# A gate carried with each sorted row, and half of the combine moved beside the last expert

## What is computed

```
mod = (silu(c) @ wmod).reshape(16, 6, 1, 128)      # sa, ca, ga, sb, cb, gb for each sequence
gb  = (2 * (gb >= 0) - 1) * maximum(abs(gb), 0.25)
h = layernorm(x) * (1 + cb) + sb
out = swiglu(h, shared_gate_up, shared_down)
probs = softmax(h @ gate_weight.T)                 # 8 experts
top_p, sel = top_k(probs, 2); top_p /= sum(top_p) + 1e-8
out += sum over the 2 picks: top_p * swiglu(h, experts_gate_up[sel], experts_down[sel])
x = x + gb * out
```

## Time and profile before

| | us |
|---|---|
| median of 3 runs | 767.89 (766.65 to 770.26) |
| the profiled execution, its own time | 766.81 |
| its span, first to last instruction | 765.0 |
| mean granted TensorE clock over the span | 0.933 |
| busy in the span: PE, DVE, ACT, POOL | 659.7, 561.0, 431.9, 375.5 |
| first part, up to the first expert tile | 0 to 401 |
| 19 expert tiles | 401 to 728 |
| last turn, last scatters, combine, output | 728 to 765 |

### The profile page before, as it was taken

How to read it: one execution, slowest core, us unless ns; L and a number is a source line. 1 busy time by engine, 2 the same in 40 slices (tenths; PEclk the granted TensorE clock), 3 DMA queues, 4 the chain that set the end, 5 groups by cost and what they waited for, 6 DMA issues and landing times.

```text
span 765.0 us, 11950 instructions
## 1 busy us (share of the span) xinstructions
PE 659.7 (86%) x3026; PEld 502.2 (66%) x3026; DVE 561.0 (73%) x1233; ACT 431.9 (56%) x822; POOL 375.5 (49%) x299
## 2 busy tenths in 40 slices
PE   5777989889998989888679999999999999999900
PEld 2455766666676667666458787778878777887800
DVE  4878978979798987976656676766776676776736
ACT  3456657575666658563345565556666665566600
POOL 1324545738456464736245473829246273832245
PEclk9797989999899999999989999999999999999955
DMA  8403001010000000000221303030401303010045
GB/s 255 99 1 98 25 5 34 21 27 28 27 24 27 18 14 27 28 27 29 84 71 28 119 26 118 28 121 30 125 16 48 112 18 118 26 35 25 28 151 188
DMA packets 41301, 44.61 MB, mean 58 GB/s; under 512 B 8052, under 2 KB 31976, under 8 KB 41280
## 3 DMA queue, kind: packets, MB, share of 16 engines
q1 hardware_dynamic: 36672, 35.89, 15.7%
q0 software_dynamic: 4608, 8.47, 3.4%
HBM read 31.62 MB, written 13.76 MB: 59 GB/s over the span
## 4 chain that ended last, share of the span: by engine, by line
PE 49%; DVE 27%; issue 12%; POOL 3%; ACT 3%; DMA 3%; DVEq 1%; POOLq 0%; SPq 0%; ACTq 0%
PE PS L619 45%; PE PS L622 4%; DVE al L1276 3%; DVE acc L1289 2%; DMA result_dram<-y_rows,aux_d 2%; DVE prod L1269 2%; DVE yT L1379 1%; DVE PS L1269 1%; DVE wd L1362 1%; POOL result_dram L578 1%; POOL pair L505 1%; POOL sorted_dram L515 1%; DVE diag L1366 1%; DVE dB L1313 1%; ACT y_sb L994 1%
## 5 line engine op out<-in xcount | busy, mean ns | idle before, releaser
L982 ACT ACTIVATE sg<-PS 128x512 f32<-128x512 f32 x216 | 129.0, 598 | 133.8 <-PE PS L619 132.3
L619 PE MATMUL PS<-xh,w_lo 128*128 128x512 f32 x405 | 176.3, 435 | 11.9 <-DVE prod L1269 7.6
L1269 DVE TENSOR_TENSOR PS<-PS,sg 128x512 f32<-128x512 f32 (+1 forms) x160 | 111.4, 697 | 94.4 <-PE PS L619 76.7
L619 PE MATMUL PS<-xl,w_hi 128*128 128x512 f32 x405 | 162.2, 400 | 0.0
L578 POOL DMA_INDIRECT result_dram<-y_rows,aux_d x80 | 78.2, 977 | 170.8 <-DVE y_rows L1644 142.3
L619 PE MATMUL PS<-xh,w_hi 128*128 128x512 f32 x405 | 161.9, 400 | 0.0
L515 POOL DMA_INDIRECT sorted_dram<-h,slot x64 | 74.0, 1157 | 90.2 <-DVE slot L1476 64.3
L619 PEld LDWEIGHTS PS<-xh,w_lo 128*128 128x128 f32 x405 | 77.9, 192 | 45.2 <-DVE prod L1269 14.2
L1276 DVE TENSOR_TENSOR al<-PS,ah 128x512 fp32r<-128x512 f32 x140 | 95.6, 683 | 8.9 <-ACT ah L990 6.2
L619 PE MATMUL PS<-ah,w_lo 128*128 128x512 f32 x216 | 94.5, 438 | 8.2 <-ACT ah L990 5.4
L990 ACT CAST ah<-PS 128x512 fp32r<-128x512 f32 (+1 forms) x160 | 92.9, 581 | 8.7 <-DVE PS L1269 7.9
(11 more groups left out here) (225 smaller groups left out, 1113.6 us busy)
## 6 DMA issues: line engine op xcount, KB each, us to landing
stage<-in_w_gu SPq DMA_DIRECT2D x18, 448.0 KB
xin<-sorted_dram SPq DMA_DIRECT2D x20, 260.0 KB, 2.7
stage<-in_w_dn SPq DMA_DIRECT2D x9, 448.0 KB
tab<-mods_dram SPq DMA_DIRECT2D x8, 384.0 KB, 3.6
sorted_dram<-pad SPq DMA_DIRECT2D x8, 260.0 KB, 2.5
out<-X SPq DMA_DIRECT2D x4, 512.0 KB, 3.2
stage<-result_dram SPq DMA_DIRECT2D x3, 512.0 KB, 4.8
result_dram<-y_rows,aux_d POOLq DMA_INDIRECT x80
```

The costliest lines, as they stand in the source:

```text
L619: return nc.tensor.matmul(out, lhsT, rhs, start=start, stop=stop, **k)
L982: A.activation(dst, src, ACT.Silu).then_inc(s["silu_done"], 1)
L1269: V.tensor_tensor(product_in(where, c)[0:n, :], bank("up", where, c)[0:n, :], sg[0:n, c % 3, :], ALU.mult).then_inc(s["prod_done"], 1)
```

## The change

- ROW becomes 258: a sorted row also carries the 128 gate values of its sequence. They are laid into `h2` by 4 broadcast DMAs for each group (`load_gates`), which SP issues once the scatters of the group before have landed. `gb_all` is gone.
- In the expert part, ACT's `split_tile` keeps the old row numbers in `aux_prev` and copies 130 columns of `xin` to `aux_next`. `move_aux` is gone. POOL forms `gw` = weight x gate for each tile (`gates`) and converts the row numbers (`results`). DVE multiplies the turned result by `gw`.
- Row numbers are now pick * 4096 + g * 512 + p * 4 + j, where pick 0 is the token's lower expert. No row of the first half comes from expert 7. The last expert always has at least 2 tiles.
- During the last expert SP loads the first half (8 DMAs of 256 KB) and POOL adds it to X, in 8 instructions of 128x512: 6 before the results of its next tile, 2 before the last results.
- At the end the second half (8 DMAs of 256 KB) is added by 8 DVE instructions, and X goes out in 8 DMAs.

```diff
-ROW = P + 2
+ROW = 2 * P + 2
...
+            def load_gates(g):
+                for k in range(2):
+                    for q in range(GS):
+                        sp.dma_start(h2[:, k, 2 * q:2 * q + 2, P + 2:ROW],
+                                     mods_dram[bass.ds(g * GS + q, 1), 3, :].unsqueeze(0).to_broadcast(
+                                         [P, 2, P])).then_inc(s["gates_in"], 16)
...
             with sp.Fori(1, G) as g:
                 sp.wait_ge(s["tab_free"], g)
                 load_tab(g)
+                sp.wait_ge(s["sorted_out"], 16 * 2 * GC * g)
+                load_gates(g)
                 sp.wait_ge(s["tab_g_free"], g)
                 load_tab_g(g)
...
+            res = result_dram.rearrange("(k g p j) d -> k g p (j d)", k=2, g=G, p=P)
+            tiles, first = tiles_of(sp, E - 1)
+            load_tile((E - 1) * REGION + TILE, first + 1)
+            sp.wait_ge(s["results_out"], 64 * (first + 2))
             for g in range(G):
-                sp.dma_start(fin[g], res[:, g * GC:(g + 1) * GC]).then_inc(s[f"final_in{g}"], 16)
+                sp.dma_start(half[g], res[0, g]).then_inc(s[f"half_in{g}"], 16)
+            with sp.Fori(0, tiles - 1) as t:
+                load_tile(next_row(E - 1, t, tiles, 2), first + t + 2)
+            count = first + tiles
+            sp.wait_ge(s["results_out"], 64 * (count + 2))
+            for g in range(G):
+                sp.dma_start(fin[g], res[1, g]).then_inc(s[f"final_in{g}"], 16)
+            for g in range(G):
+                sp.wait_ge(s["final_ready"], g + 1)
+                sp.dma_start(out_view[g], X[:, g * GC:(g + 1) * GC, :]).then_inc(s["out_done"], 16)
...
             def results(i):
 
                 pool.wait_ge(s["y_out"], SHARED + 1 + i)
+                pool.wait_ge(s["aux_read"], i + 2)
                 apart(pool)
+                V.tensor_copy(aux_d[:], aux_prev[:]).then_inc(s["aux_moved"], 1)
+                pool.wait_ge(s["aux_moved"], i + 1)
+                apart(pool)
+                scatter()
...
+            def gates(i):
+
+                pool.wait_ge(s["aux_read"], i + 2)
+                apart(pool)
+                V.tensor_tensor(gw[:], aux_next[:, :, 2:P + 2], aux_next[:, :, 0:1].to_broadcast([P, TR, P]),
+                                ALU.mult).then_inc(s["gates_ready"], 1)
...
+            def add_half(g):
+                pool.wait_ge(s[f"half_in{g}"], 16)
+                V.tensor_tensor(tokens_of(g), tokens_of(g), half[g], ALU.add).then_inc(s["half_added"], 1)
+
+            tiles, first = tiles_of(pool, E - 1)
+            for g in range(FIRST_ADDS):
+                add_half(g)
+            with pool.Fori(0, tiles - 1) as t:
+                results(first + t + 1)
+                gates(first + t + 1)
+            for g in range(FIRST_ADDS, G):
+                add_half(g)
+            results(first + tiles)
...
             def split_tile(i):
                 act.wait_ge(s["xt_done"], i + 1)
                 A.copy(xh[:], PS[:, 7, :]).then_inc(s["rh_ready"], 1)
-                act.wait_ge(s["aux_moved"], i + 1)
-                A.copy(aux_next[:], xin[:, :, P:P + 2]).then_inc(s["aux_read"], 1)
-
-            def move_aux(i):
-
-                act.wait_ge(s["results_out"], 64 * (i + 1))
-                act.wait_ge(s["aux_read"], i + 2)
-                A.copy(aux_w[:], aux_next[:, :, 0])
-                A.copy(aux_d[:], aux_next[:, :, 1]).then_inc(s["aux_moved"], 1)
+                act.wait_ge(s["gates_ready"], i + 1)
+                act.wait_ge(s["aux_moved"], i)
+                apart(act)
+                A.copy(aux_prev[:], aux_next[:, :, 1]).then_inc(s["aux_kept"], 1)
+                act.wait_ge(s["aux_kept"], i + 1)
+                A.copy(aux_next[:], xin[:, :, P:ROW]).then_inc(s["aux_read"], 1)
...
+                V.tensor_tensor(top[:, 2, :], top[:, 11, :], top[:, 10, :], ALU.is_gt)
                 link(V.tensor_reduce(top[:, 3, :], ex[:], AX.X, ALU.add))
...
-                dve.wait_ge(s["aux_moved"], i + 1)
-                V.tensor_tensor(y_rows[:], PS[:, 7, :].rearrange("p (r d) -> p r d", r=TR),
-                                bc(aux_w[:].unsqueeze(2), [P, TR, P]), ALU.mult).then_inc(s["y_out"], 1)
+                dve.wait_ge(s["gates_ready"], i + 1)
+                dve.wait_ge(s["results_out"], 64 * (i + 1))
+                V.tensor_tensor(y_rows[:], PS[:, 7, :].rearrange("p (r d) -> p r d", r=TR), gw[:], ALU.mult).then_inc(s["y_out"], 1)
...
+            for g in range(G):
+                dve.wait_ge(s[f"final_in{g}"], 16)
+                dve.wait_ge(s["half_added"], g + 1)
+                V.tensor_tensor(tokens_of(g), tokens_of(g), fin[g], ALU.add).then_inc(s["final_ready"], 1)
```

More of the change, by code:

```diff
@@ L571, in _, with scatter @@
             pool.wait_ge(s["plan_ready"], 1)
-            def results(i):
-                pool.wait_ge(s["y_out"], SHARED + 1 + i)
-                apart(pool)
+            def scatter():
                 for r in range(TR):
```

151 lines of the change are left out of this document (65 added, 86 removed).

## The result

The changed kernel takes 745.33 us (median of 4 runs, 744.27 to 747.34), the kernel before 767.27 in the same rounds: ratio 0.971, 95% interval 0.967 to 0.975. Six more runs (`e19`) gave 0.971 again (0.968 to 0.974).

A forecast was written before the change was run, and what follows sets the result against it. The prediction took PE to bound the expert part, and DVE, then the write of X's last quarter, to bound the tail. Its terms: 766.81 - 10.5 - 5.2 + 1.0 + 0.8 = 753 us, range 748 to 760.

The forecast's parts named there:

- The first part: Before the expert part: one more small DVE instruction in each of 8 passes, 0.1 us each, +0.8 us.
- The wait on landed scatters: Expert part: ACT no longer waits for scatters to land, DVE waits a tile later instead; -5.2 us.
- the new wait: Expert part: ACT waits behind `xh` for POOL's `gw`; 0.15 us in each of 7 tiles behind a split, +1.0 us.
- The tail: Behind the last tile: half the loads and two of three DVE steps per group removed, 17.2 for 28.1 us; -10.5 us.
- The delay of the scatters: Tail: the last scatters wait for one more small POOL instruction and its semaphore; +0.4 us, ends 0.2 and 1.1.
- the three terms behind it: Tail: 2.0 us before data flows, loads 5.5 and output 7.2 us, 2.5 us from last byte to end.
- The first half beside the last expert: Last expert: first-half loads and POOL's sums fit beside it; cost 0, up to 1 us if the cover is gone.
- POOL's turn as the stall: Rival, expert part: `gw` comes later still, 1.2 us of lateness reaches PE in all 7 tiles; 760 us, chance 0.13.
- The longer rows: Rival, first part: 1032-byte rows lengthen every scatter; slower, 823 us if time is proportional to bytes; chance 0.04.
- Small pieces that don't overlap: Rival, tail: each of 16 pieces of 256 KB takes its 2.7 us alone; 783 us, chance 0.02.
- The first half in the way: Rival, last expert: POOL's sums take half as long again, tile 18's `gw` 2 to 3 us late; 756 us, chance 0.06.

The follow-up runs named there:

- e19: The changed kernel unedited, run once more in more rounds beside the kernel before: 745.73 us, ratio 0.971.
- e3: The kernel before with only the change's two DVE edits of the first part (one more small instruction, row number by scalar_tensor_tensor): ratio 1.003.
- e6: The kernel before with all first-part edits: the two DVE edits, 258-float rows, gate loads and POOL's wait for them: ratio 1.005.
- e11: The kernel before with three more DVE instructions ahead of the loop, the memset of `aux_w` cut into four: 763.22 us, ratio 0.994.
- e12: The changed kernel with three of DVE's four memsets at the start moved to POOL's setup: 751.02 us, ratio 0.977.
- e9: The changed kernel without POOL's second semaphore mark behind its wait for the row numbers: ratio 0.971.
- e8: The kernel before with four more semaphore marks on POOL between its wait for the row numbers and the scatters of each pass: ratio 0.999.
- e18: The changed kernel with POOL forming `gw` twice for each tile, the second behind the first: 760.14 us, ratio 0.991.
- e15: The changed kernel with the first half loaded and added at the end, alternating with the second half, not beside the last expert: 752.98 us, ratio 0.983.
- e17: The changed kernel with POOL's `c_exp` waiting for `dl_upto` and its `low` of chunk 5 waiting for DVE's `h`: 745.35 us, ratio 0.974.

## Why the prediction was right and wrong

**The first part (+0.8 us) is the step that failed.** It measured -5.4. The term itself, an instruction more for each pass, is too small to be told from the noise in e3 and e6. What I took for granted is that the rest of the pass stays as it is. The changed kernel has three more instructions on DVE ahead of that `prod`, one of them in the loop; e11 puts three ahead of the loop of the old kernel and has the gain (5.4 us in the `h` stretch, 3.9 in the medians, ratio 0.994), e12 takes three away and loses it (5.2 and 5.7 us). So some 5 of the 7.7 us by which I missed come from this. The sum of the misses by part is 6.2 for the first part and 0.9 for the tail, less 0.3 for the tiles; the last 0.9 is that the profiled execution lies above the median of its runs (746.18 and 745.33). The text had named the mechanism, "shifts in the first part, where POOL and DVE hold each other up and a small move can turn either way", and had given it 1 us of range. The rows of before could have sized it: `dl_upto` with a mean of 1436 ns and a shortest of 224, and `c_exp` only 0.09 us ahead of it. A race that narrow, with a DVE instruction 1.7 us longer or shorter in each of the steady passes, is a case of its own with a chance of its own.

The -5.4 is made up of -5.3 in the `h` stretch, -1.7 ahead of it and +1.6 behind it (36.6 to 38.2 us from the last `h` to the first `xh`). The last two are not the change's: over all profiles the first `h` comes between 60.7 and 67.6 us, in both kernels, and the piece behind the last `h` takes 36.6 us in both profiles of before, 38.2 in e11 (before, but for the setup) and 36.6 in e9 (the changed kernel, but for a mark).

**The wait on landed scatters (-5.2) and the new wait (+1.0).** Measured together -3.9, as if the sum were right. It isn't quite: tile 0 grew from 16.79 to 18.36 us, in a stretch where the granted clock fell to 0.50, the lower of its two levels. That too comes and goes: e8, with the old rows, has 18.21, and e9, with the new ones, 16.80. In all 20 profiles tile 0 takes 16.7 to 16.8 us where the clock was 1.00 over its first 8 us (eight of them) and 18.2 to 19.2 where it was 0.79 (twelve). Without tile 0 the 18 others went from 309.4 to 304.0, so -5.4: the removed wait as predicted, the new wait 0, its lower end. e18 shows that this 0 is narrow.

**The tail (-10.5)** measured -11.4, and there some luck was in it. The delay of the scatters was taken as 0.4 and is 0.44 (1.29 for 0.85), and the order, DVE's sums beside the transfers, was right. But the three terms behind it were all off, by -1.0, +1.4 and -1.4 us, and partly cancel. Data flows 1.0 us after the first issue (728.23 to 729.18) and not 2.0. The 4.2 MB of loads and output take 14.1 us (to 743.31) and not 12.7: they overlap, and the window from 730 to 736 moves 279 GB/s, not 380; the pure output at the end runs at 345 and not at 292. The quiet end is 1.1 us and not 2.5. I had carried it over as something that follows the last byte; in the kernel before it was POOL's DRAIN, which the change took out of the way together with POOL's sums. The reading that the old tail was bound by DVE and the last write missed that.

**The first half beside the last expert (0)** was right: tile 18 takes 16.73 us, and the six sums and the scatters behind them end in time. Its worth, the 5.5 us, is 6.9 in e15's profile, of which 2.8 are POOL's DRAIN, which I didn't have in the sum.

**The rivals.** POOL's turn as the stall: not in the changed kernel, whose waits are 0.4 us at most. e18 gives that rival's 760 us, but for that `gw` had to come some 3 us later in the tiles behind a split, not 1.2. The longer rows: refuted, 1147 ns for each scatter, and e6. Small pieces that don't overlap: refuted by the windows. The first half in the way: not in its place beside the last expert, seen in e15.

## What to carry to other kernels

When an instruction has a mean far above its shortest duration, ask what it stands behind on the other engine, and by how much it lost: if by a tenth of a microsecond, any edit, even outside the loop, can turn it, and the forecast needs both outcomes. Then fix the order by a semaphore instead of leaving it to chance, so that the short instruction goes first: here one wait on GpSimd gave 14 us in the kernel before, two thirds of what the whole change gave; but look first who waits for the engine that is put back (e17). Quiet time at the end of a span is not a constant of the output: ask which engine closes last. And before counting a wait as hidden, double what causes it: the cover behind ScalarE's was 0.9 to 1.5 us and not the 2.7 that the matmuls in the queue seemed to offer.

## What the runs showed of the hardware

- A DVE instruction in a loop started 0.09 us later or earlier with the number of instructions ahead of it in DVE's program (places 225 and 226 against 228), all that DVE did before it in the pass equal to 0.01 us; in the loop's first pass the difference was 0.35 us.
- POOL's closing DRAIN ended 6.6 to 7.0 us behind POOL's last instruction in all 20 profiles. It ended the span in the kernel before (758.17 to 764.81, span 765.03) and in e15 (742.35 to 749.31, span 749.5).
- POOL starts an instruction 0.07 us behind its own result when it is a computation (`gw` to the second `gw` in e18: 433.09 + 1.06 to 434.22), but 0.86 us when it is an indirect DMA.
- An indirect DMA of 128 rows takes POOL 1147 ns with 1032-byte rows and 1157 with 520: no cost for length.
- Writes of 256 KB, several in flight, moved 345 GB/s, where the last of four writes of 512 KB, with at most two in flight, had run at 292. Whether the size or the number in flight makes the difference was not tested.
